# Zero matmuls in TensorE's waits of a kernel of attention and routed experts

## What is computed

```
x = x + attn(layernorm(x))            # (8, 512, 128)
  kv = (x @ w_kv_down) @ w_kv_up;  q = x @ w_q
  y = softmax(causal(q k' / 8)) v;  return y @ w_out
x = x + ffn(layernorm(x))
  logits = x @ Wr;  top 2 of 8 experts, weights by softmax
  h = silu(x @ Wg[e]) * (x @ Wu[e]);  out = sum_e weight_e * (h @ Wd[e]) / sqrt(12)
```

## Time and profile before

| | us |
|---|---|
| median of 3 runs | 949.34 (948.89 to 950.56) |
| profiled execution | 950.33 |
| its span, first to last instruction | 948.5 |
| TensorE busy in it | 882.4 |
| VectorE, ScalarE, GpSimd busy | 665.7, 620.1, 541.9 |

### The profile page before, as it was taken

How to read it: one execution, slowest core, us unless ns; L and a number is a source line. 1 busy time by engine, 2 the same in 40 slices (tenths; PEclk the granted TensorE clock), 3 DMA queues, 4 the chain that set the end, 5 groups by cost and what they waited for, 6 DMA issues and landing times.

```text
span 948.5 us, 20447 instructions
## 1 busy us (share of the span) xinstructions
PE 882.4 (93%) x6126; PEld 647.6 (68%) x6127; DVE 665.7 (70%) x2442; ACT 620.1 (65%) x1614; POOL 541.9 (57%) x536
## 2 busy tenths in 40 slices
PE   6799999999999999999999999999842999999996
PEld 3566666676666667676666767676522888888885
DVE  3576788878788887878888787877853444554552
ACT  3577687777768777776877777777721455445553
POOL 3455544585566558556655855665553466665555
PEclk9999999999999999999999999999975999999998
DMA  6585430000000000000000000000011233333332
GB/s 180 181 326 212 184 101 1 1 24 13 1 11 26 1 2 23 12 2 12 24 1 1 25 12 1 11 26 1 2 34 37 35 48 49 45 45 45 45 44 28
DMA packets 43996, 44.36 MB, mean 47 GB/s; under 512 B 4352, under 2 KB 35968, under 8 KB 43920
## 3 DMA queue, kind: packets, MB, share of 16 engines
q0 software_dynamic: 16528, 26.03, 11.4%
q1 hardware_dynamic: 27392, 17.39, 6.7%
HBM read 15.28 MB, written 28.12 MB: 46 GB/s over the span
## 4 chain that ended last, share of the span: by engine, by line
PE 79%; DVE 13%; POOL 4%; issue 2%; ACT 1%; DMA 0%; POOLq 0%; SPq 0%; DVEq 0%
PE low_ps L997 11%; PE low_ps L984 7%; PE low_ps L1149 7%; PE mid_ps L925 7%; DVE prob L639 6%; PE top_ps L984 6%; PE mid_ps L927 6%; PE mid_ps L926 6%; PE out_ps L1004 5%; PE mid_ps L970 4%; PE out_ps L1141 4%; PE low_ps L970 4%; PE top_ps L970 3%; DVE routed L733 2%; DVE PT L613 2%
## 5 line engine op out<-in xcount | busy, mean ns | idle before, releaser
L333 POOL TENSOR_TENSOR prob<-prob,row_inv 128x512 f32<-128x512 f32 (+3 forms) x256 | 321.6, 1273 | 263.2 <-DVE row_inv L646 263.2
L465 ACT ACTIVATE prob<-prob,neg_max 128x256 f32<-128x256 f32 (+3 forms) x512 | 280.6, 550 | 10.3 <-DVE neg_max L639 3.8
L997 PE MATMUL low_ps<-PT,v_sb 128*64 128x512 f32 (+3 forms) x1024 | 152.0, 439 | 2.1 <-ACT PT L471 1.2
L997 PEld LDWEIGHTS low_ps<-PT,v_sb 128*64 128x64 f32 x1024 | 68.1, 136 | 94.1 <-issue 60.4
L414 POOL DMA_INDIRECT out<-prob,meta_row x71 | 110.6, 1558 | 36.2 <-issue 35.7
L651 DVE COPY PT<-low_ps 128x512 f32<-128x512 f32 (+1 forms) x128 | 104.6, 817 | 31.9 <-PE low_ps L984 30.8
L984 PEld LDWEIGHTS low_ps<-ident,prob 128*128 128x128 f32 x640 | 75.2, 141 | 57.7 <-POOL prob L333 27.5
L882 DVE TENSOR_TENSOR prob<-mid_ps,prob 128x512 f32<-128x512 f32 x71 | 49.1, 692 | 91.6 <-ACT prob L570 84.6
L476 ACT ACTIVATE v_sb<-mid_ps 128x512 f32<-128x512 f32 x64 | 38.3, 598 | 103.0 <-PE mid_ps L927 102.8
L639 DVE CUSTOM_DVE_ANT_0 prob<-mid_ps,mask 128x128 f32<-128x128 f32 (+1 forms) x256 | 93.7, 421 | 6.7 <-PE mid_ps L970 0.8
L984 PE MATMUL low_ps<-ident,prob 128*128 128x128 f32 x640 | 92.2, 275 | 6.2 <-DVE PT L651 5.2
(11 more groups left out here) (172 smaller groups left out, 1773.7 us busy)
## 6 DMA issues: line engine op xcount, KB each, us to landing
routed_rows<-W_dn POOLq DMA_DIRECT2D x8, 2080.0 KB, 8.9
routed<-routed_rows SPq DMA_DIRECT2D x71, 65.0 KB, 1.9
X<-in_L_attn_x SPq DMA_DIRECT2D x8, 256.0 KB, 5.5
W_ffn<-in_L_ffn_Wg SPq DMA_DIRECT2D x8, 256.0 KB, 5.1
W_ffn<-in_L_ffn_Wu SPq DMA_DIRECT2D x8, 256.0 KB, 5.4
W_dn<-in_L_ffn_Wd SPq DMA_DIRECT2D x8, 256.0 KB, 4.6
out<-X SPq DMA_DIRECT2D x8, 256.0 KB, 2.3
out<-prob,meta_row POOLq DMA_INDIRECT x71, 3.3
```

The source lines that it names most:

```text
L333: nc.gpsimd.tensor_tensor(p_pair(i), p_pair(i), row_inv[:, i, :].unsqueeze(2).to_broadcast([P, 2, P * (i + 1)]), ALU.mult).then_inc(S["nor ...
L465: nc.scalar.activation(p_at(i, h), p_at(i, h), ACT.Exp, bias=neg_max[:, i, h:h + 1], scale=-1.0, accum_out=row_sum[:, i, h:h + 1]).then_in ...
L997: last = nc.tensor.matmul(y_ps[h * HD:(h + 1) * HD, j * P:T], v_sb[:, half, j, o + h * HD:o + (h + 1) * HD], PT[:, h, j, j:NT, :].rearrang ...
```

## The change

VectorE sets a 128x512 bf16 tile `idle_bf` to zero as its first instruction. A function `idle(ps, n)` on TensorE issues n matmuls of this tile with itself into a bank that nothing reads in that state. It is called at ten places: 5 before the first transpose of the weights, 3 behind it, 6 behind the first fold, 5 behind `pre_T(0)`, 8 behind the first projection; then 3 before `post_out` of the last sequence, 24 behind it, 4 behind `post_xn2T`, 9 behind `post_logits` and 70 behind `post_ranks`. The fillers wait for nothing but the memset, and nothing waits for them except what stands behind them on TensorE. No other engine's program changes but for the memset.

```diff
+        idle_bf = sb("idle_bf", [P, T], BF16)
...
         def _(dve):
+            nc.vector.memset(idle_bf[:, :], 0.0).then_inc(S["idle_set"], 1)
             dve.wait_ge(consts, 5)
...
         def _(pe):
+            def idle(ps, n):
+                for _ in range(n):
+                    nc.tensor.matmul(ps[:, 0:T], idle_bf[:, 0:P], idle_bf[:, :], start=True, stop=True)
+
+            pe.wait_ge(S["idle_set"], 1)
+            idle(out_ps, 5)
             pe.wait_ge(consts, 5)
             pe.wait_ge(w_in["down"], 16)
             nc.tensor.transpose(post_ps[:, 0:P], w_down_sb, ident[:, :]).then_inc(S["wdT_ready"], 1)
+            idle(out_ps, 3)
             pe.wait_ge(S["wdT_copied"], 1)
...
             fold("k0", top_ps[:, 0:T], 0)
+            idle(out_ps, 6)
             pre_T(0)
+            idle(out_ps, 5)
             pe.wait_ge(S["wlo_done"], 2)
             project(0, 0, 0)
+            idle(out_ps, 8)
             for i in ORDER:
                 scores(0, i)
...
             step(B - 1, NP, cur=False, nxt=False, v=False)
+            idle(mid_ps, 3)
             post_out(B - 1)
+            idle(mid_ps, 24)
             post_xn2T(B - 1)
+            idle(mid_ps, 4)
             post_logits(B - 1)
+            idle(mid_ps, 9)
             post_ranks(B - 1)
+            idle(mid_ps, 70)
```

More of the change, by code:

```diff
@@ L210, in layer @@
             "stats_a", "aggr_a", "rstd_a", "xn_done", "xT_ready", "xThi_done", "xTlo_done",
-            "wdT_ready", "wdT_copied", "kv_ready", "whi_done", "wlo_done",
+            "idle_set", "wdT_ready", "wdT_copied", "kv_ready", "whi_done", "wlo_done",
             "qk_ready", "qkhi_done", "qklo_done", "v_ready", "v_copied", "s_ready", "max_done", "exp_done", "inv_done", "norm_done",
```

## The result

| us | before | after |
|---|---|---|
| median of 5 runs each, same chip | 950.56 (948.89 to 951.48) | **945.35** (943.44 to 946.88) |
| ratio, 95% interval | | 0.9944 [0.9928, 0.9961] |
| profiled execution (span) | 950.33 (948.5) | 943.44 (941.6) |

A forecast was written before the change was run, and what follows sets the result against it. TensorE, busy 93% of the span, was taken to bound the kernel, slowed by low clock and long waits. Gains of 4.05 (prologue) and 4.4 (change of stages) took 950.33 to 941.9, less 0.9 for a median 941.0 us; range 939.3 to 944.6.

The forecast's parts named there:

- The clock in the prologue, 4.05: Prologue: fillers raise TensorE's clock by about 8 us, speeding transposes, projection, scores and v fold; 4.05 us gained net.
- The memset's 0.1: Prologue: VectorE's memset of the zeros may hold up GpSimd's mask fill; 0.1 us lost, at most 0.53.
- rival 2: Prologue: clock rises only at the scores, leaving transposes and most of the projection slow; 2.65 us lost, 943.7 us, 12%.
- The change of stages, 4.4: Attention to experts: full clock speeds transposes, logits, ranks and the stretch through the first tiles; 4.4 us gained.
- The 70 zeros: Wait of 16.40 us before the first tile: 70 fillers take 16.1 us at 0.23 each, covered by 0.3.
- "0.3 us or more": Sign of being right: the first tile starts near 0.3 us or more behind the last filler.
- The 8 zeros before the scores, −0.2: Before the scores: 8 fillers need 1.84 us against a cover of 1.61, costing 0.2 us.
- "Sum 8.45 … For a median I subtract 0.9": Whole kernel: 4.05 + 4.4 off the profiled 950.33 gives 941.9; less 0.9 for a median, 941.0 us.
- The stretch at 32 us: Low clock at 32 us, no filler against it: costs about 1.7 us, present in some executions of both kernels.
- rival 3: First tiles: the clock falls again in waits there, losing 2.5 us; 943.5 us, 12%.
- Rival 4: First batch: loads or GpSimd's fills swallow the prologue's gain of 4.05 us; 945 us, 5%.

The follow-up runs named there:

- layout_only: Changed kernel with tile, semaphore and memset kept but all fillers removed; 947.73 us, ratio 0.9999 to the kernel before.
- seventy_more: all_filled with 88 fillers in place of 74 ahead of the first tile; 942.67 us, ratio 0.9949 to the kernel before.
- eight_more: all_filled with 15 fillers in place of 7 ahead of the first scores; 942.07 us, ratio 0.9944 to the kernel before.
- first comparison: The changed kernel against the kernel before, 5 runs each on the same chip; 945.35 against 950.56 us, ratio 0.9944.
- all_filled: Changed kernel plus 11 fillers at 25 to 28 us, 74 for 70, 4 and 6 in first-tile waits, 7 for 8 before scores; 940.49 us, ratio 0.9924.
- after_again: The changed kernel itself, unaltered, measured again on another chip; 942.79 us, ratio 0.9952 to the kernel before.
- after_third: The changed kernel itself, unaltered, measured a third time on another chip; 941.89 us, ratio 0.9947 to the kernel before.
- seventy_gone: all_filled without the 74 fillers between the ranking and the first tile; 942.18 us, ratio 0.9945 to the kernel before.

## Why the prediction was wrong

**The clock in the prologue, 4.05.** Right for the profiled pair, term by term: transposes 0.66, projections stepping by 0.23, scores at 14.28 (14.2 forecast), split at 18.18 (18.2), 4.11 us in all. The memset's 0.1 was nothing: layout_only has it and its prologue is that of before up to 13.68 us. The first zeros ran and the clock was up at 8.8 us, so rival 2 did not occur in this trace. A mild form of it did in seventy_more's, with transposes 1.1 us late, though rival 2 wanted 2.65.

**The change of stages, 4.4.** Right too for that pair: 4.3. Transposes 0.66, logits 1.03 (0.96), 4.45 us from the first tile to its transposes (4.3), 2.90 to the next (2.88). The 70 zeros took 15.27 us in place of 16.1, and 1.19 us of the wait were left ("0.3 us or more"). (The clock row has three slices below 9, not two; no term rests on the third, the last one.)

**The 8 zeros before the scores, −0.2.** Right in kind: beyond the wait they have no cover. eight_more's scores start 1.73 us later for 8 zeros, 0.216 each, and its time is 1.58 us longer.

**"Sum 8.45 … For a median I subtract 0.9": the step that failed.** It failed in two ways.

In the profiled pair the forecast was 941.9 with the fall at 32 us, so 940.2 without it, as in the trace; 943.44 came. Both terms are there in full. But 2.93 us were lost in attention, where VectorE's row minima were late, and for that stretch the sum has no term at all.

Over executions the two terms are not properties of the kernel. Both were differences to one execution, and I took everything in it but the stretch at 32 us as given. How soon TensorE's clock rises by itself in the prologue and in the first tiles differs from execution to execution of the same work. layout_only's trace has 1.47 us to gain in the prologue where mine had 4.1 (1.69 and 4.35, less the 0.22 that the changed kernel has there). Measured over 12 runs, each part is worth 2.6 and 2.9 us, not 4.05 and 4.4; the 4.05 lies outside its interval, the 4.4 just inside (1.4 to 4.5), while the sum, 8.45, lies outside the intervals of the whole change in all three comparisons (at most 6.8). Rival 2 held against the zeros that before "the transposes and the projection with their waits did not raise it"; that was one execution's outcome. The Trainium skill, page "TensorE: Matmul & The Clock Gate", section "What's actually happening", says that the point at which the clock rises varies from run to run, with the phase at which the kernel starts. That it varies the traces show (up by the scores at 15.7 us in one, only at some 21 us in two); the phase no run shows. The page's advice to leave such a ramp out as under 1% doesn't help where the whole change is 0.6%.

How the miss of 4.35 us (945.35 for 941.0) divides between the two is open. In the first comparison the profile of before was no outlier, 950.33 at a median of 950.56, while that of the changed kernel was the fastest of its five, 1.9 us below the median, and no trace shows what the other four had.

**The stretch at 32 us.** "Present in some executions and absent in others" was right, "no filler against it" too. Its price of 1.7 was right as well (1.4 to 1.7), and so was it to subtract only half of it for a median. What the sum lacks are the other falls that the changed kernel has in some executions, those at the first tiles: rival 3, put at 12% as a state of the kernel and at 2.5 us, is something that comes and goes and cost 1.9 to 2.1. all_filled shows the price over runs: closing the holes gives 0.9924 against 0.9944, 0.9952 and 0.9947, some 2 to 2.6 us, with intervals that just part from the second and overlap with the others.

**Rival 4** (945, the prologue's gain swallowed) named the right time for a wrong reason. It wanted loads or GpSimd's fills in the first batch to do it. What swallowed 2.9 us in the profiled execution were the late minima, in attention, with the prologue's gain intact up to the first of them. The gain over the kernel before is as small without them: the traces of after_again and after_third have none, and their ratios are the same within the intervals.

**What stays open.** Why the minima were late in that execution. It was seen in 1 of 14 profiled executions, in the first comparison, whose times are some 3 us higher for both kernels; the kernel before was profiled without it. The unprofiled runs don't tell how many of them had it. The Trainium skill, page "SBUF — State Buffer", section "SBUF: two separate sides", has a lock by which VectorE and GpSimd wait for each other, for some forms of instruction. The forms that it names for VectorE are those in a two-port mode or with two inputs in SBUF; this minimum has one input in PSUM and one in SBUF, and no run shows its mode. A lock held for the whole of GpSimd's instruction would fit the three minima that start just behind it (281.29 and 280.29 + 0.96), but not the nine that start within it (187.26), nor that the same pair overlaps in the other 13 traces. Nor was it tried what the rise and fall of the clock hangs on within an execution.

## What to carry to other kernels

Zeros in TensorE's waits are worth what the low clock costs on average, so look at several executions before you price a low stretch: a single profile may show the worst one. Fill every wait near the path, not only those that show a fall in your trace, up to the wait's length and no further: beyond the wait 8 fillers too many cost 1.6 us of the time and 14 cost 2.2, most of their 0.216 us each. Where the clock is low a filler takes 0.43 us, and a cover worked out at 0.23 breaks. The spread of the runs is a measure of its own: in one comparison it was 3.6 us for the kernel before, 2.1 for the changed one and 0.5 with the last holes filled.

## What the runs showed that I had not expected

- The same wait of 2.53 us ahead of the transposes at 28 us is followed by a fall of the clock in some executions (1.51 us for six transposes) and not in others (0.85).
- A fall came at 685 us too, where the profile before had TensorE busy for 2.25 of 5 us at a clock of 1.00.
- One execution in which a VectorE instruction out of PSUM comes 0.33 to 0.98 us late near a GpSimd DMA with indices, 12 times of 12, three times up to the end of that DMA's instruction, while in 13 others it never does.
- Ten zeros put into waits at the low clock made the stretch longer: 9.41 us from the first tile to the second transposes of h in seventy_gone, 8.15 in two traces without them.
